# The last rows of an attention and expert layer: statistics on another engine, and a new order of work around them

## The reference

```python
q, k, v = fq(split(ln(x) @ Wq + bq) * scale), fq(...), fq(...)    # symmetric, 127 steps
attn = fq_unsigned(softmax(q @ k.T))                                # 255 steps of the row's maximum
x = x + (attn @ v) @ Wp + bp
y = ln(x)
inh = sigmoid(y @ Wr / temperature)
distance = |inh - 1/e|
weights = exp(-distance / 0.1) * (GOLDEN_LOWER <= inh <= 0.5)       # or the two nearest experts, if none is in the zone
weights = weights / sum(weights)
out = x + sum_e weights[e] * ((silu(y @ Wg[e]) * (y @ Wu[e])) @ Wd[e])
```

## Time and profile before

| | us |
|---|---|
| median of 3 runs | 740.18 (739.73 to 742.54) |
| profiled execution, its own time | 740.93 |
| its span, first to last instruction | 739.2 |
| PE busy | 626.5 (85%) |
| VectorE busy | 567.8 (77%) |
| ScalarE busy | 459.6 (62%) |
| GpSimd busy | 405.0 (55%) |
| TensorE's mean granted clock | 0.977 of full |

### The profile page before, as it was taken

The page is one execution under the profiler, slowest core; times in us unless marked ns, Lnnn a source line. Parts: engine busy times, 40 slices in busy tenths (PEclk is TensorE's granted clock), DMA queues, the critical chain, the costliest instruction groups (busy, mean ns, idle before and its releaser), DMA issues. The chain is left out here.

```text
span 739.2 us, 15774 instructions
## 1 busy us (share of the span) xinstructions
PE 626.5 (85%) x5298; PEld 326.8 (44%) x5298; DVE 567.8 (77%) x919; ACT 459.6 (62%) x552; POOL 405.0 (55%) x457
## 2 busy tenths in 40 slices
PE   7999999666767777786867777899999999999992
PEld 3444443233433444343434355455555555555551
DVE  4997778999999999999999995783746637456330
ACT  6334358588978989898989897243534435344321
POOL 5254457546677878787878773225334443354403
PEclk9999999899999999999999998899999999999997
DMA  6777867999999999999999995359796887977804
GB/s 245 198 149 168 167 142 123 191 172 158 185 159 186 195 182 198 183 199 187 193 188 190 189 176 129 115 188 200 204 250 122 240 234 175 247 166 199 135 5 57
DMA packets 317492, 129.16 MB, mean 175 GB/s; under 512 B 292484, under 2 KB 292484, under 8 KB 317448
## 3 DMA queue, kind: packets, MB, share of 16 engines
q1 hardware_dynamic: 310272, 112.38, 71.4%
q0 software_dynamic: 7168, 16.26, 10.8%
q10 hardware_dynamic: 8, 0.01, 0.0%
HBM read 44.33 MB, written 12.06 MB: 76 GB/s over the span
## 5 line engine op out<-in xcount | busy, mean ns | idle before, releaser
L998 ACT ACTIVATE work<-spare,exp_bias 128x2048 uint8<-128x2048 f32 (+1 forms) x128 | 255.1, 1994 | 31.6 <-POOL exp_bias L656 22.2
L1319 DVE TENSOR_SCALAR_CACHE_REDUCE spare<-psum,q_step_now 128x1024 f32<-128x1024 f32 x128 | 162.4, 1272 | 2.4 <-PE psum L1733 2.4
L650 POOL CAST work<-work 128x2048 int16<-128x2048 uint8 x71 | 134.2, 1890 | 33.4 <-DMA work<-work 20.7
L1310 DVE TENSOR_SCALAR_CACHE_REDUCE spare<-psum,q_step_now 128x2048 f32<-128x2048 f32 x64 | 150.2, 2347 | 0.6 <-PE psum L1733 0.5
L1733 PE MATMUL psum<-keys_region,work 128*128 128x512 f16 x256 | 74.2, 391 | 44.8 <-DVE spare L1319 24.6
L781 POOL DMA_INDIRECT work<-x_rows,slot_tok x32 | 50.9, 1591 | 96.2 <-DVE slot_w L1507 73.1
L1733 PE MATMUL psum<-keys_region,bias_hl 128*128 128x512 f16 x256 | 70.6, 381 | 29.1 <-DVE spare L1319 22.9
L793 POOL DMA_INDIRECT out_dram<-keys_region,slot_tok x32 | 51.7, 1617 | 74.0 <-ACT keys_region L1077 67.0
L1693 PEld LDWEIGHTS psum<-values_region,work 128*128 128x128 f16 x2048 | 65.8, 96 | 36.5 <-POOL work L650 20.6
L1693 PE MATMUL psum<-values_region,work 128*128 128x32 f16 x2048 | 70.7, 177 | 11.5 <-POOL work L650 7.0
L1575 PE MATMUL psum<-work,spare 128*128 128x480 f16 (+1 forms) x396 | 79.2, 360 | 0.9 <-DVE work L1480 0.9
(11 more groups left out here) (223 smaller groups left out, 1020.0 us busy)
## 6 DMA issues: line engine op xcount, KB each, us to landing
spare<-in_L_ffn_Wd_dram SPq DMA_DIRECT2D x8, 1024.0 KB, 15.3
spare<-in_L_ffn_Wg_dram SPq DMA_DIRECT2D x7, 1024.0 KB, 5.8
spare<-in_L_ffn_Wu_dram SPq DMA_DIRECT2D x7, 1024.0 KB, 9.9
work<-in_ctx_dram SPq DMA_DIRECT2D x3, 1024.0 KB, 5.9
work<-work SPq DMA_TRANSPOSE x174, 3.6
token_region<-in_L_xattn_Wkv_dram SPq DMA_DIRECT2D x2, 1024.0 KB, 6.5
resid<-in_x_dram SPq DMA_DIRECT2D x2, 1024.0 KB, 8.6
out_dram<-work SPq DMA_DIRECT2D x8, 256.0 KB, 2.6
```

The source lines that it names most:

```text
L650: nc.gpsimd.tensor_copy(p_T_int[h % 4], pair_bytes[h % 4]).then_inc(unpacked, 1)
L998: nc.scalar.activation(p_out, scores, ACT.Exp, bias=exp_bias[:, h % 4:h % 4 + 1], scale=-1.0, accum_out=p_sum[:, h:h + 1]).then_inc(exp_do ...
L1310: nc.vector.tensor_scalar(staged[h % 4], psum[:, at:at + 4, :].rearrange("p b k -> p (b k)"), q_step_now[:, h:h + 1], None, ALU.mult, ALU.min,
L1319: nc.vector.tensor_scalar(staged[h % 4][:, 1024 * c:1024 * c + 1024], psum[:, at:at + 2, :].rearrange("p b k -> p (b k)"), q_step_now[:, h ...
```

## The change

In all tiles with rows to handle, SP transposes the rows of tile i - 2 behind head 11 of the attention rather than head 10. In the last tile GpSimd adds the residual of tile 6 at head 13 rather than 12, so behind one bias and one unpacking. The statistics of tile 6 leave ScalarE (`square_rows`, `normalise_rows`) and GpSimd (`deviation_begun`, `deviation_ended`): VectorE makes them with `bn_stats`, and normalises the rows, ahead of its copies of head 14. ScalarE does `cut_rows(6)` and `exp_logits(0)` ahead of its four copies of head 15. VectorE does `closeness(0)` ahead of `divide`. On PE, tile 5's logits come behind four filler products and the values of heads 11 and 10, and two fillers between the turning of heads 14 and 15 go.

```diff
@@ transpose_tile (SP)
-                    if h == 10 and after_rows:
+                    if h == 11 and after_rows:
                         turn_rows(i - 2)
@@ attention_tile (GpSimd)
                 if not following:
-                    add_at, half_at = 12, 13
+                    add_at, half_at = 13, 13
@@ behind it
             attention_tile(QT - 1, True, False)
-            deviation_ended(QT - 2, deviation_begun(QT - 2))
             rows_low(QT - 2)
@@ ScalarE
-            square_rows(QT - 2)
+            cut_rows(QT - 2)
+            exp_logits(0)
             for g in range(DK):
                 act.wait_ge(probs_turned[1], g + 1)
                 nc.scalar.activation(last_T[1][:, 512 * g:512 * g + 512], bank(PROB_BANKS[1][g]), ACT.Copy, scale=SUBNORMAL).then_inc(probsT_out[1], 1)
-            exp_logits(0)
             act.wait_ge(att_ready, 2 * QT)
             nc.scalar.activation(att_hl[:, 1, 0, :], att[:, 256:512], ACT.Copy).then_inc(att_hi, 1)
-            normalise_rows(QT - 2)
             for l in range(2):
...
-            cut_rows(QT - 2)
             act.wait_ge(exp_done, H * QT)
@@ VectorE
             nc.vector.tensor_scalar(ident, column[:, :], slot_now[:, 0:1], None, ALU.is_equal).then_inc(ident_ready, 1)
+            dve.wait_ge(x1_added, QT - 1)
+            dve.wait_ge(x1_cut, QT - 2)
+            own.link(nc.vector.bn_stats(ln1_stats[:, 0, :], x1))
+            own.link(nc.vector.bn_aggr(ln1_mv[:, :], ln1_stats[:, 0, :]))
+            own.link(nc.vector.tensor_scalar(var, ln1_mv[:, 1:2], LN_EPS, None, ALU.add))
+            rsqrt(own, var, y, t)
+            nc.vector.tensor_scalar(x1_norm, x1, ln1_mv[:, 0:1], y, ALU.subtract, ALU.mult).then_inc(x1_normed, 1)
             for g in range(DK):
...
             invert_sums(QT - 1, 1)
+            closeness(0)
             divide(QT - 1, 1)
...
-            closeness(0)
             compare(0)
@@ logits (PE)
+                    if t == QT - 3:
+                        pe.wait_ge(scores_taken, 2 * H * QT - 2)
+                        keep_busy(2, 4)
+                        for h in (H - 5, H - 6):
+                            values(QT - 1, h, True)
+                        pe.wait_ge(x1T_in, 16 * (QT - 2))
@@ PE, behind the attention
-            pe.wait_ge(x1T_in, 16 * (QT - 2))
+            pe.wait_ge(x1T_in, 16 * (QT - 3))
             logits(0)
-            for h in (H, H + 1):
-                values(QT - 1, h - (7 if h % 2 else 5), True)
             pe.wait_ge(scores_taken, 2 * H * QT)
             pe.wait_ge(ident_ready, 1)
             turn_probs(0)
-            keep_busy(4, 2)
             turn_probs(1)
```

## The result

The kernel became slower by a third of a per cent: 744.33 us in the median of 18 runs (742.0 to 748.15) against 742.51 (739.73 to 744.89) of the kernel before in 18, ratio 1.0034, 95% interval 1.0019 to 1.0049, so +2.5 us (the two medians by themselves lie 1.8 apart). The profiled execution has a span of 744.3 us and a mean granted clock of 0.972. Every execution behind the ratios of this document was a fast one; the only slow one, 1221.65 us in early_fill, is left out of its ratio.

A forecast was written before the change was run, and what follows sets the result against it. The path through head 15's copies, `divide` and the last projection was taken to bound the kernel. Terms +1.2 - 0.8 - 0.55 and clock +1.25 gave +1.1 on 740.18: 741.3 us, own range 740.5 to 742.2, wider range 738.3 to 743.3.

The forecast's parts named there:

- What bounds, and the path: Between attention and experts, some 35 us with no engine full; a chain through head 15's copies, `divide`, `add_projection`, `cut_rows(7)` bounds.
- rigidly: Claim that all behind the path to the last scatter hangs on it, so every us saved comes off the end.
- ScalarE behind `divide`: -0.8 and -0.55: Without `normalise_rows(6)`, turned-attention copies start 0.8 us earlier; `cut_rows(7)`, no longer held by tile 6's store, gains 0.55.
- ScalarE ahead of `divide`: +1.2: `cut_rows(6)` ahead of head 15's copies waits for tile 5's store, landing at 449.2; `divide` 1.2 us later (0.9 to 1.6).
- priced at 0: SP's `turn_rows` one head later in tiles 2 to 7: nothing waits for it in the loop, 0 us.
- VectorE at no cost: Twelve more VectorE instructions (3.4 us) ahead of its copies cost nothing under ScalarE's wait, 0.7 us without that cover.
- PE at no cost and no gain: PE's new order turns head 15 1.1 to 1.5 us earlier, worth 0 as ScalarE waits for the store.
- The clock, +1.25: PE idles ahead of head 15's values, so its clock falls for one of two projection halves: +1.25 us (0 to 2.8).
- rival 3: Clock falls before head 15's values end and stays low in the second projection: +2.65 us, 742.8; chance 0.10.
- Rival 1: Same wait for the store but no fall of PE's clock: -0.15 us, 740.0; chance 0.25.
- rival 2: Store lands before 447 and is not last; `divide` 1.7 us earlier, in all -3.1 us, 737.1; chance 0.12.
- The sum: Whole kernel: -0.15 us without the clock, +1.1 us with it, set on the median of 740.18.

The follow-up runs named there:

- early_fill: As close_fill, but `closeness(0)` ahead of `divide` as in the changed kernel; ratio to the kernel before 0.9978.
- again: The changed kernel without any edit, timed on another occasion; ratio to the kernel before 1.0046, median 742.56 us.
- orders_only: The kernel before with only the change's new orders on PE, SP and GpSimd, ScalarE and VectorE as before; ratio to the kernel before 1.0010.
- stats_only: The kernel before with only tile 6's statistics and normalising moved to VectorE, other orders as before; ratio to the kernel before 1.0002.
- close_back: As store_early, but `closeness(0)` on VectorE again behind the cut of the attention; ratio to the kernel before 0.9987.
- close_fill: As close_back, plus 6 filler products of 512 columns on PE behind the values of heads 11 and 10; ratio to the kernel before 0.9969.
- fill_gap: The changed kernel with 12 filler products of 512 columns on PE between the values of heads 14 and 15; ratio to the kernel before 1.0023.
- store_early: The changed kernel, but in the last tile SP stores tile 5's rows behind head 10's transposition; ratio to the kernel before 0.9980, median 738.14 us.
- cut_behind: The changed kernel, but ScalarE does `cut_rows(6)` behind its four copies of head 15 again; ratio to the kernel before 0.9976.
- turn_at_10: The changed kernel with `turn_rows` behind head 10 again in all tiles; ratio to the kernel before 1.0015.
- store_late: The changed kernel, but in the last tile tile 5's rows are stored behind the output of tile 6's rows; ratio to the kernel before 1.0054.

## Why the prediction was right or wrong

**What bounds, and the path.** Right. The chain of waits of the kernel after runs through the store, the four copies and the projection. The last column of the table moves with the ratio over 14 profiles. But "rigidly" was too strong for what lies behind: from `cut_rows(7)` to the first copy of gathered rows it is 16.2 us in the profile before, 18.4 in that of the changed kernel and 17.0 in again. Much of the difference is a wait of VectorE for `slot_w`, 4.1 us long in five profiles (the changed kernel, orders_only, stats_only, close_back, close_fill) and 1.1 to 2.3 in the others. It comes and goes between two profiles of one kernel, so it is no part of the change, and its cause is open.

**ScalarE behind `divide`: -0.8 and -0.55.** Right, and seen where the clock does not cover them: in fill_gap `add_projection` follows `divide` by 3.12 (predicted 3.90 - 0.80 = 3.10), and from there to `cut_rows(7)` it is 4.44 against 460.51 - 455.51 = 5.00 us; its release is VectorE's, no DMA's.

**ScalarE ahead of `divide`: +1.2, this is the step that failed in size.** The wait was named and it is the cause (store_early, cut_behind). But `divide` came 2.5 us later, not 1.2. The copies' own way from the landing was as worked out (449.73 to 452.55: 2.82 against 0.05 + 0.52 + 0.28 + 2.06 = 2.91). The place of the landing was not: I had it at 449.2, 7.0 behind the mark, with a bound at 449.6; it came 8.3 behind the mark. I let head 13's earlier exponential bring the store forward by 0.4 to 0.7 us, and bounded it by its old place "as the transpositions ahead of it are as many bytes". Neither held. The exponential did end 0.6 us earlier, but nothing of that reached the store: `turn_rows`, one head later and priced at 0, kept SP's queue, and head 13's transposition began to issue where it had before (turn_at_10, with `turn_rows` back, stores 0.6 earlier). And as many bytes took longer: that transposition was issued in 3.56 us instead of 2.44, the attention's in 1.19 instead of 1.45, so the store went off 6.1 behind the mark instead of 5.2. The first part is shown; for the second, the pause behind a load of instructions is likely and not shown. The time from issue to landing was right: 2.18 us in the chain of waits. The Trainium skill, page "DMA: Bandwidth & Descriptors", section "Anatomy of one DMA — SWDGE (gpsimd) path", led to an estimate of 2.6 for it; the section's fit is for DMAs that GpSimd issues, and this store is issued by the sync engine, so the measured 2.18 goes ahead of it and says nothing against it.

**VectorE at no cost.** Its rows came at 446.0, 4.6 behind the mark (predicted 4.8), but there was an instruction of 0.68 and one of 1.15 us among those of 0.15 to 0.22. They cost nothing under the wait for the store. Without it they do (store_early, early_fill), where I had the price without the cover at 0.7: too little, since I counted the moved `closeness(0)` at nothing (close_back, with it behind, has `divide` 0.55 earlier).

**PE at no cost and no gain.** Right, as far as its own work goes: head 15 was turned by 447.7 and nobody used it for 2.8 us. With the store out of the way its gain appears: the copies end 1.4 us earlier than before.

**The clock, +1.25.** Right in size (4.49 and 4.36 against 3.12) and one of the two projections, though the idle time was 3.38 us, where I had 2.3, and the fall came early: 0.50 at 452 to 455, as rival 3 asks, but the second twelve had the clock back and took 1.58. Rival 3's 2.8 was too dear. Rival 1 did not happen in the two profiles; rival 2 is what store_early made: 16.4 against 18.3 behind the mark, -1.9 where I had -3.1. The difference lies ahead of `divide`, at 8.9 instead of 9.4 - 1.7 = 7.7, and 0.87 of it is VectorE's stretched instruction; behind `divide` it is 7.5 against 8.9, the predicted 1.35.

**The sum.** With the measured terms: +2.5 - 0.8 - 0.55 + 1.35 = +2.5 us, the same as the ratio gives (+1.8 between the medians). Predicted +1.1. The range of 738.3 to 743.3 missed 744.33 for two reasons. One is the landing of the store, 1.3 us later than I had it, so that the term of +1.2 measured +2.5. The other is its base, as the median of 740.18 in three runs became 742.51 in eighteen: 2.3 us, where I had allowed 1 for a median although the three runs lay 2.8 apart. Of the 3.0 us between 741.3 and 744.33 the base has 2.3, so without it the time would have stood in the range in spite of the failed step.

## What to carry to other kernels

When a step is moved ahead in an engine's hand-written order, list its old waits one by one: one that was free at the old place (here the landing of a store, free because the cut came 5 us later) can be the last at the new one, and everything queued behind it pays. The repair is to move what is waited for, or to put the waiting step behind the work it blocks; both gave 4.4 us here. And do not bound a DMA's issue by its old time because the bytes ahead are the same: count from a mark, follow the queue's own order (a DMA moved one place later holds all behind it), and take the slowest issue of the same kind for the upper bound. In the profile before, 55 transpositions like head 13's took 1.92 us to issue in the median and 2.94 at most; that would have put the bound 0.5 later, at 7.9 behind the mark, nearer to the 8.3 though still short of it.

## What the runs showed of the hardware

- DMAs of transpositions nearly stand still behind a load of instructions: in the kernel after for 1.3 us (442.75 to 444.1) behind a load of 0.02 MB at 442.4, and for 0.65 us (445.1 to 445.75) behind one of 0.01 MB at 444.55. The second load and pause are in all twelve profiles with the twelve more instructions on VectorE and in neither of the two without; which engine's instructions it brings, no run shows.
- Small instructions of VectorE on 1 or 48 columns, which take 0.14 to 0.22 us otherwise, took 0.67 to 1.86 us once or twice in each kernel with the new statistics between 440 and 465 us (1.86 in stats_only, 1.83 in early_fill), and never there in the kernel before and in orders_only. Whether a load of instructions stretches them was not tested.
- The first of two stores of 256 KB issued some 0.6 us apart landed 2.2 to 2.3 us behind its issue in all nine profiles that have the pair. The second took 2.3 to 2.7 us in four of them and 4.1 to 4.4 in five (4.4 in store_late); what decides is open.
